# Work moved between places in two engine programs: slot matmuls, index arithmetic and the passage to the expert blocks

## The chip, the cores and the metric

The kernel runs on one core of a Trainium2 chip. The metric is the device time of one execution in microseconds. Five engines run their own instruction queues beside one another: TensorE (PE), VectorE (DVE), ScalarE (ACT), GpSimd (POOL) and SyncE (SP), which here only starts DMAs. They wait for one another by semaphores.

## The reference, cut to what matters

```
x: [32 sequences, 256 tokens, 128]
xn  = layernorm(x)
out = x + attention(xn) + experts(xn)

attention, per sequence (4 heads, keys 32 wide, values 64 wide, chunks of 64):
    q, k, v, g = xn @ Wq, xn @ Wk, xn @ Wv, xn @ Wg
    decay = cumulated log_sigmoid(xn @ Wgk + bgk) / 16
    o  = causal (q k^T * exp(decay differences)) v     # with a state carried on
    on = o * rsqrt(mean(o*o) + eps) * gnorm_w
    attention = (on * g * sigmoid(g)) @ Wo

experts (8), per token, the one with the largest router probability:
    h = gelu(xn @ w1[e] + b1[e]);  y = h @ w2[e] + b2[e]
    experts = probability * y
```

## The kernel before

**Three stages.** The first loads x, transposes it and works out norm statistics, decays and router logits. The second, the attention stage, takes the 32 sequences one by one, two to a turn of a loop. The third takes the tokens, sorted by expert into 71 blocks of 128 rows, eight to a turn.

**A step of the attention stage** (sequence s) on TensorE, in this order: transpose of the keys (L778), query and key projections of s+1 (L757), scores of s (L790), output projection of s-2 (L859), value and gate projections of s+1 (L771, six matmuls of 512 columns), state of s (L814), outputs of s (L825, L839), transpose of the normalized rows of s-1 (L851). ScalarE turns the results into decays (L1148), tanh (L1130), copies (L1139, L1122, L1164) and squares (L1157). Vector, in its own order: gate (L1546), low part of x (L1331), mean square (L1471, L1475), probabilities (L1509), decayed keys (L1515), gated outputs (L1521), scaled queries (L1494), normalized rows (L1529), copy of the state (L1537), residual (L1554). GpSimd takes the inverse root of the mean squares (L561) and masks the decays (L554). Scores of s wait for the gate of s, since they share a PSUM bank, and the value projections of s+1 wait for the first half of the probabilities of s.

**The sort in between.** Beside sequences 2 to 8, small work finds each token's place: TensorE counts tokens and makes their slots (`count_tokens`, `count_totals`, `block_ends`, `slots`, L737 to L742), Vector reads these and works out positions and the expert of each block (`read_ends`, `slots_to_positions`, `past_ends` L1455, `count_past` L1459, `block_experts` L1462). These are hooked into Vector's step at named places: `aside` (ahead of the probabilities), `behind_keys`, `read` (behind the state's copy) and `behind` (at the end). From step 5 to 29 GpSimd also places the rows: each of 64 indirect DMAs (L577) writes 128 rows to sorted memory; `placed_by` sets two or three a step. SP loads the sorted rows (L461) once all placements have landed.

**A block of the last stage**: Vector copies the expert's first-layer weights and biases (`copy_w`, L1669) and normalizes the gathered rows (`norm_rows`, L1676); TensorE transposes them (L956), ScalarE copies the transpose (L1263), TensorE runs the first layer (L965), ScalarE the gelu (L1274), TensorE the second layer (L977), for which it reads the expert's number from memory into a register of its queue (L983); Vector adds the bias and weighs (L1685, L1687), and GpSimd adds the rows to the output with an indirect DMA (`scatter`, L619). The scatters begin only once the attention results of all sequences are stored (SP, L397), because they add to the same rows. `weigh` also copies the row numbers (L1683).

**Orders written out by hand.** There is no planner. Where the attention stage ends and the blocks begin, the code lists each engine's calls by hand: `transpose_on(last, 1)`, `project_out(last, 1)` and `residual(last, 1)` are the last sequence's, `layer1(0, j)`, `layer2(0, j)`, `weigh(0, j)` those of block j.

Of the kernel before, what the change touches and what calls it, by code (L numbers as in the profile page):

```python
# [33 lines left out]
def turn(i, j, d, n):  # L34

    return i + (j + d) // n, (j + d) % n
# [27 lines left out]
def build_layer(nc, x, Wq, Wk, Wv, Wg, Wgk, bgk, Wo, gnorm_w, gate_w, w1, b1, w2, b2, out):  # L64
# [18 lines left out]
    R = 8  # L83
# [21 lines left out]
    with ExitStack() as ctx:  # L105
# [533 lines left out]
        def _(pe):  # L639
# [222 lines left out]

            def step(i, j, extra=None, ahead_of_outputs=None):
                first_keys(i, j)
                proj_qk(*turn(i, j, 1, 2))
                scores(i, j)
                project_out(*turn(i, j, -2, 2))
                if extra:
                    extra()
                proj_vg(*turn(i, j, 1, 2))  # L870
                state(i, j)
                if ahead_of_outputs:
                    ahead_of_outputs()
                outputs(i, j)
                transpose_on(*turn(i, j, -1, 2))
# [63 lines left out]
            step(1, 1, extra=count_totals)  # L939
            step(2, 0, extra=block_ends, ahead_of_outputs=slots)  # L940
            step(2, 1)
# [40 lines left out]
            def expert_of(b):  # L982
                return pe.value_load(be[0:1, bass.ds(b, 1)], min_val=0, max_val=EXP - 1)  # L983

            def block_step(i, j):
                layer1(i, j)
                e = expert_of(i * R + j - 1)
                if not (isinstance(i, int) and i * R + j + 1 >= BLOCKS):
                    transpose_rows(*turn(i, j, 1, R))
                layer2(*turn(i, j, -1, R), e)  # L990

# [16 lines left out]
            transpose_rows(0, 2)  # L1008
            layer1(0, 2)
            transpose_on(last, 1)  # L1010
            transpose_rows(0, 3)
            layer2(0, 1, expert_of(1))
            project_out(last, 1)
            for j in range(3, R):
                block_step(0, j)
            for i in range(1, TURNS - 1):
# [8 lines left out]
        def _(act):  # L1025
# [261 lines left out]
            copy_oT(last, 0)  # L1287
            copy_rows(0, 1)
            copy_rows(0, 2)
            gelu(0, 1)  # L1290
            copy_oT(last, 1)
# [12 lines left out]
        def _(dve):  # L1304
# [251 lines left out]

            def step(i, j, aside=None, behind_keys=None, read=None, behind=None):
                s = i * 2 + j
# [4 lines left out]
                if inside(i, j, -1, SEQS):  # L1563
                    mean_square(*turn(i, j, -1, 2))
                if aside:
                    aside()
                if inside(i, j, 0, SEQS):
                    probs(i, j)
                    decay_k(i, j)
                if behind_keys:  # L1570
                    behind_keys()
                if inside(i, j, -1, SEQS):
# [70 lines left out]
            dve.wait_ge(act_decay, 2 * DECAY_N)  # L1643
            step(2, 0, aside=weights, behind_keys=read_ends, behind=slots_to_positions)
            step(2, 1, aside=past_ends)
            step(3, 0, aside=count_past)
            step(3, 1, aside=block_experts)
            step(4, 0)
            step(4, 1)
# [65 lines left out]
            e = expert_of(0, 3)  # L1715
            mean_square(last, 1)
            gated(last, 1)
            residual(last, 0)
            normed(last, 1)
            norm_rows(0, 3)  # L1720
            copy_w(0, 3, e)
            e = expert_of(0, 4)
            weigh(0, 0)
            e = block_step(0, 1, e)
            residual(last, 1)
            for j in range(2, R):
                e = block_step(0, j, e)
# [17 lines left out]
def placed_by(s):  # L1745

    n = 0
    for k in range(PLACE_FROM, min(s, PLACE_TO) + 1):
        n += 3 if k % 2 == 0 or k in (PLACE_FROM, PLACE_TO) else 2
    return n  # L1750
# [26 lines left out]
```

## Time and profile before

| | us |
|---|---|
| median of 3 runs | 389.69 (388.78 to 390.25) |
| the profiled execution, its own time | 390.25 |
| its span on the core | 388.5 |

| engine | busy us | share of the span |
|---|---|---|
| TensorE | 367.9 | 95% |
| VectorE | 312.5 | 80% |
| ScalarE | 291.5 | 75% |
| GpSimd | 276.0 | 71% |

The shares are means over all stages. In a timeline each row is one instruction or a merged group: its start, how long it took, engine and line, what it writes and reads, and in brackets how long the engine stood idle before it and which instruction ended the wait. The chain of waits starts at the last instruction and follows back, at each step, to what released it; a row of it is a start, a time on the chain, and the instruction.

### The profile page before, as it was taken

Reading aid. Unit: us, or ns where it says so; the run is one execution under the profiler, and the core shown is the slowest. Engines: PE = TensorE matmul, PEld = TensorE weight load, DVE = VectorE, ACT = ScalarE, POOL = GpSimd, SP = SyncE. Lnnn points to the kernel's source line nnn. Section 1 sums busy time; section 2 is a strip of 40 time slices with the busy share of each in tenths; the row PEclk is TensorE's granted clock in tenths of the full one; section 3 lists DMA queues with packets and bytes.
Section 4 is the critical chain, followed back from the end, with each engine's and each line's share of the span. In section 5 each row is a group of like instructions: output and inputs, shape, how many; then the busy total and the mean of one; then the engine's idle time right before and its main releaser. Section 6 shows DMA issues by size and latency. Waiting matters only on the chain.

```text
span 388.5 us, 13868 instructions
## 1 busy us (share of the span) xinstructions
PE 367.9 (95%) x3947; PEld 318.3 (82%) x3947; DVE 312.5 (80%) x859; ACT 291.5 (75%) x889; POOL 276.0 (71%) x245
## 2 busy tenths in 40 slices
PE   6997899999999999999999999999999999999980
PEld 5665677778787888888887877999999999999980
DVE  4898799988889889898889888777768778777750
ACT  3798886879898888989898985676666666666650
POOL 8002453788788888888888873288888888888883
PEclk9998999999999999999999999999999999999995
DMA  8945679556665536665663522255555555555430
GB/s 229 241 157 150 202 228 339 142 175 187 175 205 162 159 127 172 165 196 185 174 187 121 169 57 69 52 71 73 74 66 70 66 70 72 68 72 75 60 32 0
DMA packets 59106, 51.45 MB, mean 132 GB/s; under 512 B 7200, under 2 KB 51392, under 8 KB 59072
## 3 DMA queue, kind: packets, MB, share of 16 engines
q1 hardware_dynamic: 45936, 42.07, 38.6%
q0 software_dynamic: 12272, 8.54, 15.6%
q10 hardware_dynamic: 864, 0.40, 0.4%
q8 instruction: 20, 0.33, 0.3%
q14 instruction: 14, 0.11, 0.1%
HBM read 33.14 MB, written 18.30 MB: 132 GB/s over the span
## 4 chain that ended last, share of the span: by engine, by line
PE 82%; DVE 6%; ACT 4%; issue 3%; POOL 2%; DMA 2%; SPq 0%; DVEq 0%; ACTq 0%; POOLq 0%
PE psVG L965 16%; PE psA L977 16%; PE psVG L771 11%; PE psT L859 8%; PE psO L825 7%; PE psQK L757 5%; PE psT L851 4%; PE psVG L790 4%; PE psO L839 3%; PE psKS L814 3%; ACT E L1148 2%; POOL out_dram L619 2%; DMA x_all<-in_L_attn_x_dram 2%; PE psA L647 1%; DVE stats L1313 1%
## 5 line engine op out<-in xcount | busy, mean ns | idle before, releaser
L619 POOL DMA_INDIRECT out_dram<-yw,sidx x71 | 111.9, 1577 | 28.8 <-DVE yw L1687 10.3
L1148 ACT ACTIVATE E<-gcB,ngc 128x128 f32<-128x128 f32 x256 | 78.3, 394 | 0.0
L577 POOL DMA_INDIRECT sorted_rows<-x_all,pos_i x64 | 63.9, 998 | 13.4 <-issue 9.8
L561 POOL TENSOR_TENSOR rms<-msn,neg_half 128x8 f32<-128x8 f32 x32 | 53.5, 1673 | 24.5 <-DVE msn L1475 20.9
L554 POOL TENSOR_SCALAR_AFFINE_SELECT E<-E 128x1024 f32<-128x1024 f32 x32 | 35.1, 1097 | 37.4 <-ACT E L1148 28.6
L1130 ACT ACTIVATE th<-psVG,x_all 128x256 f32<-128x256 f32 x64 | 26.8, 470 | 21.4 <-PE psVG L771 20.7
L825 PE MATMUL psO<-v_sb,pr 128*64 128x64 f32 x1024 | 36.3, 225 | 2.7 <-DVE pr L1504 2.7
L977 PE MATMUL psA<-xT_all,v_sb 128*128 x288 | 38.1, 275 | 0.4 <-DVE yb L1685 0.4
L965 PE MATMUL psVG<-xgT,gcB 128*128 128x128 f32 x288 | 38.0, 275 | 0.0
L977 PE MATMUL psA<-xT_all,th 128*128 x280 | 37.5, 277 | 0.1
L825 PEld LDWEIGHTS psO<-v_sb,pr 128*64 128x64 f32 x1024 | 34.8, 141 | 3.4 <-issue 3.2
L965 PE MATMUL psVG<-xgT,E 128*128 128x128 f32 x280 | 37.1, 275 | 0.4 <-ACT xgT L1263 0.4
L859 PE MATMUL psT<-wo_sb,oT 128*128 128x128 f32 x256 | 36.9, 287 | 0.3 <-ACT oT L1164 0.3
L977 PEld LDWEIGHTS psA<-xT_all,v_sb 128*128 128x128 f32 x288 | 35.0, 192 | 0.6 <-issue 0.6
L965 PEld LDWEIGHTS psVG<-xgT,gcB 128*128 128x128 f32 x288 | 35.0, 192 | 0.0
L977 PEld LDWEIGHTS psA<-xT_all,th 128*128 128x128 f32 x280 | 34.0, 192 | 0.8 <-issue 0.6
L965 PEld LDWEIGHTS psVG<-xgT,E 128*128 128x128 f32 x280 | 34.1, 192 | 0.6 <-ACT xgT L1263 0.6
L859 PEld LDWEIGHTS psT<-wo_sb,oT 128*128 128x128 f32 x256 | 31.0, 191 | 4.1 <-ACT oT L1164 0.5
L1546 DVE SCALAR_TENSOR_TENSOR gate<-th,psVG 128x512 f32<-128x512 f32 x32 | 22.0, 686 | 9.9 <-ACT v_sb L1139 9.8
L771 PE MATMUL psVG<-w_hi,x_hi 128*128 128x512 f32 x64 | 28.0, 437 | 1.6 <-DVE pr L1509 0.9
L1263 ACT COPY xgT<-psQK 128x128 f32<-128x128 f32 x36 | 9.5, 265 | 24.2 <-PE psQK L956 24.2
L1676 DVE TENSOR_SCALAR xgn<-xg 128x128 f32<-128x128 f32 x71 | 27.1, 381 | 0.0
(209 smaller groups left out, 951.3 us busy)
## 6 DMA issues: line engine op xcount, KB each, us to landing
gcB<-decay_rows SPq DMA_DIRECT2D x32, 512.0 KB, 4.5
sorted_rows<-blank SPq DMA_DIRECT2D x12, 396.0 KB, 5.7
xg<-sorted_rows SPq DMA_DIRECT2D x71, 66.0 KB
x_all<-in_L_attn_x_dram SPq DMA_DIRECT2D x16, 256.0 KB, 5.7
out_dram<-res SPq DMA_DIRECT2D x32, 128.0 KB
eqB<-decay_exp_rows SPq DMA_DIRECT2D x32, 64.0 KB
w1b<-in_L_ffn_w_dram SPq DMA_DIRECT2D x8, 256.0 KB
xT_all<-in_L_ffn_w_dram SPq DMA_DIRECT2D x32, 64.0 KB
```

Of the source, the lines that this page charges most:

```text
L554: nc.gpsimd.affine_select(out=E[j][:], in_=E[j][:], pattern=[[0, 2 * H], [1, P]], compare_op=ALU.is_ge, fill=0.0, base=0, channel_multipli ...
L561: nc.gpsimd.tensor_tensor(rms[:], msn[:], neg_half[:, 0:2 * H], ALU.pow).then_inc(rms_ready, 1)
L577: nc.gpsimd.indirect_dma_start(out=sorted_dram, out_offset=bass.IndirectOffsetOnAxis(ap=pos_i[:, t:t + 1], axis=0), in_=x_all[:, t, :], in ...
L619: nc.gpsimd.indirect_dma_start(out=out_rows, out_offset=bass.IndirectOffsetOnAxis(ap=sidx[j][:], axis=0), in_=yw[j][:], in_offset=None, bo ...
L771: last = nc.tensor.matmul(psVG[:, k, :], xp[:, k * P:(k + 1) * P], wp[:, 2 * P:], start=(n == 0), stop=(n == 2))
L825: nc.tensor.matmul(psO[c * P // 2:(c + 1) * P // 2, k * HV + h * DV:k * HV + (h + 1) * DV], pr[:, h // 2, t:t + P // 2], v_sb[j][:, k, h * ...
L859: last = nc.tensor.matmul(psT[:, k * D:(k + 1) * D], oT[:, 2 * k + a, :], wo_sb[:, a, :], start=(a == 0), stop=(a == 1))
L965: last = nc.tensor.matmul(psVG[:, j % 2, c * P:(c + 1) * P], wbuf[j % 4][:, c * P:(c + 1) * P], xgT[j % 2][:], start=True, stop=True)
L977: last = nc.tensor.matmul(psY[j % 2][:, 0:D], hid[j % 2][:, c, :], w2_sb[:, bass.ds(e, 1), c, :].rearrange("p a d -> p (a d)"), start=(c = ...
L1130: last = nc.scalar.activation(th[:, k, :], psVG[:, k, HV:2 * HV], ACT.Tanh, scale=x_all[:, bass.ds(s * 2 + k, 1), D + 2:D + 3].rearrange(" ...
L1148: last = nc.scalar.activation(E[j][:, k, h * P:(h + 1) * P], gcB[j][:, k * H + h, :], ACT.Exp, bias=ngcf[:, bass.ds((s * 2 + k) * H + h, 1)])
L1676: nc.vector.tensor_scalar(xgn[j % 4][:], xg[j][:, 0:D], xg[j][:, D + 2:D + 3], xg[j][:, D + 3:D + 4], ALU.mult, ALU.add).then_inc(xgn_read ...
```

## The change

Five edits: (1) TensorE's `slots` in step 4 stands ahead of `state` instead of behind it. (2) On Vector the `aside` work stands behind the decayed keys instead of ahead of the probabilities; the place `behind_keys` is gone, and `read_ends` moves behind the state's copy; `past_ends`, `count_past` and `block_experts` move to later places. (3) GpSimd places two groups instead of three in step 5 and three instead of two in step 27. (4) In the passage, TensorE runs the first layer of block 2 and the row transpose of block 3 after `project_out(last, 1)`, not around `transpose_on(last, 1)`; ScalarE runs the gelu of block 1 ahead of the row copy of block 2. (5) There Vector runs the weight copy and row norm of block 3 ahead of the last normalized rows, and `residual(last, 1)` ahead of what belongs to block 1's step.

```diff
@@ TensorE
-            def step(i, j, extra=None, ahead_of_outputs=None):
+            def step(i, j, extra=None, behind_vg=None):
...
                 proj_vg(*turn(i, j, 1, 2))
+                if behind_vg:
+                    behind_vg()
                 state(i, j)
-                if ahead_of_outputs:
-                    ahead_of_outputs()
                 outputs(i, j)
...
-            step(2, 0, extra=block_ends, ahead_of_outputs=slots)
+            step(2, 0, extra=block_ends, behind_vg=slots)
...
-            def block_step(i, j):
+            def block_step(i, j, back=True):
                 layer1(i, j)
-                e = expert_of(i * R + j - 1)
+                if back:
+                    e = expert_of(i * R + j - 1)
                 if not (isinstance(i, int) and i * R + j + 1 >= BLOCKS):
                     transpose_rows(*turn(i, j, 1, R))
-                layer2(*turn(i, j, -1, R), e)
+                if back:
+                    layer2(*turn(i, j, -1, R), e)
...
             layer1(0, 1)
             transpose_rows(0, 2)
-            layer1(0, 2)
             transpose_on(last, 1)
-            transpose_rows(0, 3)
             layer2(0, 1, expert_of(1))
             project_out(last, 1)
-            for j in range(3, R):
-                block_step(0, j)
+            for j in range(2, R):
+                block_step(0, j, back=(j > 2))
@@ ScalarE
             copy_rows(0, 1)
+            gelu(0, 1)
             copy_rows(0, 2)
-            gelu(0, 1)
             copy_oT(last, 1)
@@ Vector
                 if inside(i, j, -1, SEQS):
                     mean_square(*turn(i, j, -1, 2))
-                if aside:
-                    aside()
                 if inside(i, j, 0, SEQS):
                     probs(i, j)
                     decay_k(i, j)
-                if behind_keys:
-                    behind_keys()
+                if aside:
+                    aside()
...
-            step(2, 0, aside=weights, behind_keys=read_ends, behind=slots_to_positions)
-            step(2, 1, aside=past_ends)
-            step(3, 0, aside=count_past)
-            step(3, 1, aside=block_experts)
-            step(4, 0)
+            step(2, 0, aside=weights, read=read_ends, behind=slots_to_positions)
+            step(2, 1)
+            step(3, 0, behind=past_ends)
+            step(3, 1, behind=count_past)
+            step(4, 0, aside=block_experts)
...
             residual(last, 0)
+            copy_w(0, 3, e)
+            norm_rows(0, 3)
             normed(last, 1)
-            norm_rows(0, 3)
-            copy_w(0, 3, e)
             e = expert_of(0, 4)
             weigh(0, 0)
-            e = block_step(0, 1, e)
             residual(last, 1)
-            for j in range(2, R):
+            for j in range(1, R):
                 e = block_step(0, j, e)
@@ GpSimd's placements
-        n += 3 if k % 2 == 0 or k in (PLACE_FROM, PLACE_TO) else 2
+        n += 3 if k % 2 == 0 or k >= PLACE_TO - 2 else 2
```

## Rows read from the trace of the kernel before

**Rows 1.** Chain of waits, 45 to 92 us: start, us on the chain, instruction

```profile
62.58 1.64 PE psVG L771 x6
...
66.00 1.08 PE psO L825 x32
...
70.72 1.65 PE psVG L771 x6
...
77.60 1.66 PE psVG L771 x6
```

**Rows 2.** Chain of waits, 210 to 232 us, a step of the steady loop

```profile
222.85 1.40 PE psVG L771 x6
```

**Rows 3.** Timeline of GpSimd, scatters of blocks 0, 56 and 70 of 71

```profile
249.83 1.79 POOL L619 DMA_INDIRECT out_dram<-yw,sidx  x1 [7.52 <-DVE yw L1687]
...
355.49 1.56 POOL L619 DMA_INDIRECT out_dram<-yw,sidx  x1 [0.30 <-DVE sidx L1683]
...
381.53 1.56 POOL L619 DMA_INDIRECT out_dram<-yw,sidx  x1 [0.30 <-issue]
```

**Rows 4.** Timeline of Vector, weighed rows of block 56

```profile
352.87 0.29 DVE L1687 TENSOR_SCALAR yw<-yb,xg 128x128 f32<-128x128 f32 x1
```

**Rows 5.** Line L619, 248 to 250 us: queue instruction, ns min/median/max, first and last start

```profile
L619 POOLq MOVE  x2: 29/29/29, 249.0 to 249.7; - x2
```

**Rows 6.** Timeline of Vector, 64 to 77 us, steps 4 to 6

```profile
64.74 0.42 DVE L1537 TENSOR_TENSOR S_sb<-psKS,headmask 128x256 f32<-128x256 f32 x1
...
66.03 0.42 DVE L1419 TENSOR_TENSOR slot_f<-psA,onehot 128x256 f32<-128x256 f32 x1 [0.21 <-PE psA L742]
...
67.44 0.69 DVE L1546 SCALAR_TENSOR_TENSOR gate<-th,psVG 128x512 f32<-128x512 f32 x1
...
76.16 0.66 DVE L1459 TENSOR_REDUCE be_f<-isge 128x71 f32<-128x497 f32 x1
```

**Rows 7.** Timeline of TensorE, scores of step 5 and projections in step 6

```profile
68.85 0.38 PE L790 MATMUL psVG<-qk_sb 32*128 32x128 f32 x2
...
77.60 0.50 PE L771 MATMUL psVG<-w_hi,x_hi 128*128 128x512 f32 x1 [0.34 <-DVE pr L1509]
```

**Rows 8.** Timeline of Vector, probabilities in a steady step

```profile
102.15 0.69 DVE L1509 TENSOR_TENSOR pr<-psVG,E 128x512 f32<-128x512 f32 x1 [0.34 <-PE psA L790]
```

**Rows 9.** Timeline of GpSimd, root behind step 27, placement of step 28

```profile
215.32 1.67 POOL L561 TENSOR_TENSOR rms<-msn,neg_half 128x8 f32<-128x8 f32 x1 [0.68 <-DVE msn L1475]
...
218.53 0.96 POOL L577 DMA_INDIRECT sorted_rows<-x_all,pos_i  x1 [0.30 <-DVE on L1529]
```

**Rows 10.** Chain of waits, 240 to 252 us, the passage to the blocks

```profile
242.34 0.12 PE psQK L956
...
242.81 1.16 PE psVG L965 x8
243.97 0.44 PE psT L851 x4
...
244.63 1.16 PE psA L977 x8
...
247.69 0.89 PE psA L977 x8
...
249.58 0.89 PE psA L977 x8
```

**Rows 11.** Timeline of Vector, 232 to 247 us, the passage to the blocks

```profile
232.21 0.92 DVE L1669 COPY gcB<-w1b 128x644 f32 x1
...
242.77 0.69 DVE L1529 TENSOR_TENSOR on<-og,rms 128x512 f32<-128x512 f32 x1 [0.86 <-POOL rms L561]
...
243.63 0.49 DVE L1669 COPY E<-w1b 128x644 f32 x1
...
246.72 0.42 DVE L1554 TENSOR_TENSOR res<-psT,x_all 128x256 f32<-128x256 f32 x1 [0.28 <-PE psT L859]
```

**Rows 12.** Line L983, 243 to 244.6 us: TensorE's queue reads an expert's number

```profile
L983 PEldq TENSOR_LOAD <-be x1: 310/310/310, 243.8 to 243.8; - x1
```

More of the change, by code:

```diff
@@ L1555, in residual, with step @@
                                         ALU.add).then_inc(res_ready, 1)
-            def step(i, j, aside=None, behind_keys=None, read=None, behind=None):
+            def step(i, j, aside=None, read=None, behind=None):
                 s = i * 2 + j
```

## The prediction

> **What bounds the kernel now.** I read the chain of waits in order of time first. From 45 to 230 us it runs almost wholly on TensorE, one sequence after another; a step's six value/gate projections take 1.40 us there when nothing interrupts the engine [rows 2]. In the first steps of that stretch they take 1.64 to 1.66 us: the engine had run dry ahead of them and refills for about 0.25 us, and at 77.60 it had also waited [rows 1]. So a wait of TensorE costs its own length and a quarter of a microsecond.
>
> The second view is GpSimd's timeline. The block stage looks bound by TensorE in the shares, but the 71 scatters stand back to back, with only the 0.30 us between two that every one has: first start 249.83, last 381.53, a mean distance of 131.70 / 70 = 1.881 us [rows 3]. TensorE's own pace is nearly the same: the second layers of two blocks that follow each other start at 247.69 and 249.58, 1.89 apart [rows 10]. Scatter 56 starts at 355.49, and its row was ready at 352.87 + 0.29 = 353.16 [rows 3, 4]: a backlog of 2.33 us. Block 56 is the first of a turn of Vector's loop, where Vector falls back a little; of the stage's 71 blocks it has the least backlog. So the end is set by when the scatters start, and that is by the store of the last attention result: Vector's last residual ends at 246.72 + 0.42 = 247.14, GpSimd's queue gets past its wait at 249.0, the scatter begins at 249.83 [rows 11, 5, 3]. From residual to scatter 2.69 us, of which 0.8 lies behind the wait. That 0.8 us is also the least backlog that a scatter can have without GpSimd standing still.
>
> **Part 1, slots ahead of state (step 4).** No matmul is added or removed. Between the projections' end, 62.58 + 1.64 = 64.22, and the outputs at 66.00 lie the four state and twelve slot matmuls, 1.78 us in either order [rows 1]. What moves is Vector. Its copy of the state stood at 64.74, under the slot matmuls; now the state comes out at about 66.00, so the copy starts at 66.05. Behind it wait the read of the block ends, a residual and the slot reads, for which I take the distances between starts in the same view, 0.34, 0.19 and 0.33. First slot read 66.05 + 0.34 + 0.19 + 0.33 = 66.91, second 67.25 (before: 66.03). From second read to the next gate it was 67.44 - 66.03 = 1.41 [rows 6], so the gate of step 5 starts at 68.66 instead of 67.44 and ends at 69.35. TensorE's scores of step 5 wait for it; they stood at 68.85 [rows 7]. Loss: 69.40 - 68.85, **0.55 us**.
>
> **Part 2, the index work of Vector moved.** The comparison, count and cast leave the place ahead of the probabilities. In step 5 this pays back at once: the probabilities come 0.7 us sooner after the gate, TensorE's projections no longer wait and don't refill. They start at 70.66 + 0.55 = 71.21 and take 1.40, end 72.61, against 70.72 + 1.65 = 72.37 [rows 1, 2]: 0.24 late. In step 6 the count (0.66 at 76.16, 0.7 with the wait for its result) is gone from in front of the probabilities [rows 6]. TensorE had idled 0.34 [rows 7] and refilled to 77.60 + 1.66 = 79.26. Now: without wait 77.60 - 0.34 = 77.26, plus 0.24, plus 1.40 = 78.90. So from here on the kernel is **0.36 us ahead**. The comparison and the count, 0.7 us each, now stand ahead of the gates of steps 7 and 8, where Vector idles 0.3 for the value copy and again 0.34 ahead of the probabilities [rows 8], and TensorE needs these another 0.3 later: just covered. If not, 0.1 plus a refill of 0.25, once or twice. Sum early: -0.36, bounds -0.6 and +0.55 (nothing recovered).
>
> **Part 3, a placement from step 5 to step 27.** It costs 0.96 + 0.30 [rows 9]. In step 5 GpSimd has room. In step 27 it idles 0.68 ahead of the root [rows 9]; steps 26 to 29 now hold three each, so GpSimd is up to 0.5 late there and the last placement 0.35 late. The first gathered rows are needed only after Vector's weight copy of 232.21, which no load feeds [rows 11], and SP's loads of these rows, which wait for the last placement, come 0.35 late at most. I take 0, bounds 0 and +0.4.
>
> **Part 4, the passage to the blocks.** The last normalized rows are ready at 242.77 + 0.69 = 243.46 either way, since Vector waited 0.86 for GpSimd's root; the weight copy (0.49) and row norm (0.34) now lie inside that wait [rows 11]. Before, TensorE filled the time with the first layer of block 2 (242.81, 1.16) and transposed at 243.97. Now it has nothing between the row transpose at 242.34 and 243.52: an idle 1.1 us [rows 10]. Then four transposes (0.6), the second layer of block 1, the output projection. The second layer needs an expert number read into a register on TensorE's own queue. That read stood at 243.8 and took 0.31 [rows 12], and the matmuls began at 244.63 [rows 10], 0.83 after it. The transposes are queued at once when the rows are ready, so the read now starts at about 243.6 and the second layer at 244.43: only 0.2 earlier, though the transposes end at 244.1. Everything behind keeps its distance: residual 246.52, first scatter 249.63, **-0.20 us**. Bounds: -0.57 (read hidden), +0.15 (below).
>
> The rows transpose of block 3 now stands directly in front of its first layer, with nothing in between: transpose, copy by ScalarE, restart, as at 242.34 to 242.81, 0.47, and 0.27 of refill (1.16 against 0.89) [rows 10]. TensorE: second layer 244.43 + 1.16 = 245.59, projection to 246.48, first layer of block 2 to 247.37, transpose 0.11, layer 3 from 247.95 to 249.11, transpose 0.11, second layer of block 2 at about 249.25, against 247.69 [rows 10]: **1.56 us later**. This is the price of what was brought forward, and the backlog pays it: at block 56 it was 2.33, becomes 2.33 - 1.56 - 0.20 = 0.57, and the least is 0.8. So GpSimd stands still about **0.25 us** there. The earlier turns begin with a larger backlog, so I take nothing there.
>
> **Sum.** -0.36 - 0.20 + 0.25 = -0.3 us. The profiled execution took 390.25 (span 388.5 and 1.75 around it), the highest of the three; it would take 389.95. Against the median of 389.69 that is **389.4 us**.
>
> Vector's weight copy of the same form took 0.92 at 232.21, beside GpSimd's mask, and 0.49 at 243.63, beside no GpSimd work [rows 11]. It now stands beside the last root: if held to its end, the rows come 0.15 late. The Trainium skill says so too (GPSIMD Engine Reference, Key points): the two engines share their SBUF interfaces, and Vector's two-port modes contend. By that rule the sum would be -0.15; if the root leaves the port free, -0.3.
>
> Of the register read the Trainium skill gives a floor of some 600 ns (DMA: Bandwidth & Descriptors, Latency and other measured facts). The trace has 0.83 to the matmul, so the measurement decides; by the page's figure alone the first scatter would be 0.2 earlier still. Both agree that such a read is not free, and it speaks against this order.
>
> **Rivals.**
> 1. *The register read is hidden.* For: in steady blocks nothing is lost at it. Against: here the queue stands before it until 243.46. Then scatters start 0.57 earlier, TensorE is only 1.2 late, and block 56 again limits: -0.8 in all, 388.9.
> 2. *The stall in step 5 stays* (slower). For: the gate of step 5 is 1.2 us late, and the root and the mask follow from it, GpSimd's work too. Against: the removed count is longer than what is left. It decides if the probabilities of step 6 miss 77.1. Then +0.55 stays: +0.55 - 0.20 + 0.25, with 390.2 as a time.
> 3. *The blocks' compute becomes the bound.* For: only 0.57 of backlog left at block 56. If the restart costs 0.5 more than I worked out, or Vector falls back further at boundaries, GpSimd waits 0.5 to 1 at each such place: +0.8, 390.5.
> 4. *The scatters' own pace shifts.* The last one took 1.56, with the 0.30 ahead of it 1.86, the first 1.79 [rows 3]: it depends on how they fall against Vector's work, and with a backlog changed by 1.8 they fall elsewhere. As far above the mean of 1.881 as 1.86 lies below it is 1.90. 70 distances at 1.86 are 130.2, at 1.90 133.0, against 131.7: -1.5 to +1.3 on the forecast, 387.9 to 390.7.
>
> **Chances.** Forecast 0.43, rival 1 0.15, rival 2 0.14, rival 3 0.12, rival 4 0.16. The range goes from rival 4's low end to its high end with a little for the median's own scatter (388.78 to 390.25 before): 387.7 to 391.0. About 0.5%, 1.9 us, is what a measurement of this kernel tells from no change. Below 387.7 I put 0.10 (rival 4's low end, with 1), above 391.6 0.05, the rest 0.85.
>
> **What would show it.** Right: TensorE waits some 0.5 us ahead of the scores of step 5 and not ahead of the projections of step 6; in the passage it idles over 1 us ahead of the last transposes and again ahead of block 3's first layer; the last residual 0.2 earlier relative to the rows of 243.46; a smaller backlog of scatters, nearly none at block 56. Wrong: a residual over 0.5 earlier (rival 1), a later projection in step 6 (2), scatters that wait for Vector in many blocks (3), or a mean distance far from 1.88 (4).

## The result and the profile after

| | before | after |
|---|---|---|
| median of 7 runs | 389.47 us (388.56 to 391.76) | 392.53 us (392.00 to 393.25) |
| profiled execution, its own time / span | 390.25 / 388.5 | 391.56 / 389.8 |

The ratio is 1.0074, with an interval of 1.0048 to 1.0099: the change makes the kernel slower by 0.74%. The forecast of 389.4 and its range up to 391.0 were wrong, in size and in sign.

The shares tell nothing of it. From the page of after, busy us, share of the span and count of each engine:

```profile
PE 368.7 (95%) x3947; PEld 319.1 (82%) x3947; DVE 312.4 (80%) x859; ACT 292.0 (75%) x889; POOL 277.2 (71%) x245
```

So the two traces are cut at events that both have. The profiled pair differs by 1.31 us; what comes before step 3, which the change doesn't touch, was 1.14 us shorter in after's execution (the projections in step 2 stand at 47.82 against 48.96; this part varies from run to run). From there on after is 2.45 us longer. The projections for sequence s+1 run in step s, so those for sequences 4 and 9 run in steps 3 and 8:

| stretch | before | after | difference | predicted |
|---|---|---|---|---|
| projections for sequence 4 to those for sequence 9 | 34.43 | 35.29 | +0.86 | -0.36 |
| to those for sequence 26 | 107.11 | 107.15 | +0.04 | 0 |
| to those for sequence 31 | 31.58 | 32.23 | +0.65 | 0 |
| to the end of the last normalized rows | 13.20 | 13.23 | +0.03 | 0 |
| to the end of the last residual | 3.68 | 3.44 | -0.24 | -0.20 |
| to the first scatter | 2.68 | 2.69 | +0.01 | 0 |
| first to last scatter | 131.70 | 132.82 | +1.12 | +0.25 |

**The early stretch.** Vector after, steps 4 to 7 (answers to [rows 6]), and first the comparison in before:

```profile
69.18 0.67 DVE L1455 TENSOR_TENSOR isge<-iota_f,ends 128x497 f32<-128x497 f32 x1
```

```profile
64.87 0.42 DVE L1537 TENSOR_TENSOR S_sb<-psKS,headmask 128x256 f32<-128x256 f32 x1 [0.87 <-PE psKS L814]
...
67.47 0.69 DVE L1546 SCALAR_TENSOR_TENSOR gate<-th,psVG 128x512 f32<-128x512 f32 x1
...
79.15 1.94 DVE L1455 TENSOR_TENSOR isge<-iota_f,ends 128x497 f32<-128x497 f32 x1
81.13 0.69 DVE L1546 SCALAR_TENSOR_TENSOR gate<-th,psVG 128x512 f32<-128x512 f32 x1
...
86.39 0.66 DVE L1459 TENSOR_REDUCE be_f<-isge 128x71 f32<-128x497 f32 x1
```

GpSimd beside it:

```profile
79.45 1.10 POOL L554 TENSOR_SCALAR_AFFINE_SELECT E<-E 128x1024 f32<-128x1024 f32 x1
80.73 1.21 POOL L577 DMA_INDIRECT sorted_rows<-x_all,pos_i  x1 [0.18 <-issue]
...
86.03 1.10 POOL L554 TENSOR_SCALAR_AFFINE_SELECT E<-E 128x1024 f32<-128x1024 f32 x1
```

And the chain of waits of the same stretch (answers to [rows 1]):

```profile
67.59 0.67 issue
68.26 0.38 PE psVG L790 x2
...
70.08 1.64 PE psVG L771 x6
...
76.61 1.47 PE psVG L771 x6
...
79.58 1.52 DVE isge L1455
81.13 0.70 DVE gate L1546
```

The state copy idled 0.87 us, and the scores of step 5 waited 0.67 for the gate: part 1 as forecast. Two steps later stands what was not: the comparison, 0.67 us long in before, took 1.94, from 79.15 to 81.09. GpSimd's mask ran from 79.45 to 80.55 over it. The gate behind it starts at 81.13 and the chain leaves TensorE for it. The count at 86.39 lay beside a mask too (86.03 to 87.13) and took its 0.66: it reads one array where the comparison reads two.

**The last steps.** Vector's low part of x in steps 28 and 29, in before and in after, and GpSimd's mask in each step of after:

```profile
213.77 0.42 DVE L1331 TENSOR_TENSOR x_lo<-xT_all,x_hi 128x256 fp32r<-128x256 f32 x1
...
220.07 0.82 DVE L1331 TENSOR_TENSOR x_lo<-xT_all,x_hi 128x256 fp32r<-128x256 f32 x1
```

```profile
213.53 1.14 DVE L1331 TENSOR_TENSOR x_lo<-xT_all,x_hi 128x256 fp32r<-128x256 f32 x1
220.14 1.16 DVE L1331 TENSOR_TENSOR x_lo<-xT_all,x_hi 128x256 fp32r<-128x256 f32 x1
```

```profile
213.28 1.10 POOL L554 TENSOR_SCALAR_AFFINE_SELECT E<-E 128x1024 f32<-128x1024 f32 x1
...
219.90 1.11 POOL L554 TENSOR_SCALAR_AFFINE_SELECT E<-E 128x1024 f32<-128x1024 f32 x1
```

With three placements in each of steps 26 to 29 GpSimd is late, and its mask slides over this operation, which also reads two arrays. The mean squares and the probabilities stand behind it in Vector's order, and TensorE's projections wait for the probabilities; so the chain of waits leaves TensorE in step 28 and in step 29 (answers to [rows 2], where a group that hadn't run dry took 1.40):

```profile
213.53 0.47 DVE x_lo L1331
...
215.61 0.70 DVE pr L1509
...
216.36 1.68 PE psVG L771 x6
...
222.97 1.67 PE psVG L771 x6
```

**The passage.** TensorE after, 243 to 250 us (answers to [rows 10]):

```profile
243.95 0.65 PE L851 MATMUL psT<-ident,on 128*128 128x128 f32 x4 [1.10 <-DVE on L1529]
244.82 1.15 PE L977 MATMUL psA<-xT_all,th 128*128 x8 [0.22 <-issue]
...
248.22 1.16 PE L965 MATMUL psVG<-xgT,E 128*128 128x128 f32 x8 [0.36 <-ACT xgT L1263]
...
249.35 1.15 PE L977 MATMUL psA<-xT_all,v_sb 128*128 x8
```

The idle time of 1.1, the 0.2 us behind the transposes for the register read, the second idle time ahead of block 3: all as written. In this execution everything here stands 0.43 us later than in before (the rows are ready at 243.89 instead of 243.46), so block 2 is compared from the rows: its weighed rows come 7.29 us behind them instead of 5.77, 1.52 later.

**The scatters.** GpSimd after, first scatter, blocks 23 to 26, and the last (answers to [rows 3]); then Vector's weight copies beside them:

```profile
250.02 1.65 POOL L619 DMA_INDIRECT out_dram<-yw,sidx  x1 [7.27 <-DVE sidx L1681]
...
293.70 1.55 POOL L619 DMA_INDIRECT out_dram<-yw,sidx  x1 [0.30 <-issue]
295.55 1.81 POOL L619 DMA_INDIRECT out_dram<-yw,sidx  x1 [0.30 <-DVE yw L1685]
297.67 1.59 POOL L619 DMA_INDIRECT out_dram<-yw,sidx  x1 [0.30 <-issue]
...
382.84 1.55 POOL L619 DMA_INDIRECT out_dram<-yw,sidx  x1 [0.30 <-issue]
```

```profile
293.70 0.53 DVE L1667 COPY gcB<-w1b 128x644 f32 x1
295.12 0.49 DVE L1667 COPY gcB<-w1b 128x644 f32 x1
296.79 0.49 DVE L1667 COPY E<-w1b 128x644 f32 x1
298.69 0.49 DVE L1667 COPY E<-w1b 128x644 f32 x1
```

The idle times between the 71 scatters sum to 21.3 us in before and after alike, 0.30 each: GpSimd waited for no block. What grew is the scatters, and only some of them: it hangs on where a weight copy starts against the scatter. At 295.55 one starts 1.24 us behind the scatter's start (296.79), and the scatter takes 1.81; at 297.67 one starts 1.02 behind (298.69), and it takes 1.59; at 293.70 one starts with it and one 1.42 behind, and it takes 1.55. In the profiles of all the kernels here together 101 scatters took over 1.65 us, and beside every one of them a copy starts either 0.03 to 0.13 us ahead of the scatter or 1.05 to 1.24 us behind its start; of the scatters with such a copy only two took less, 1.62 and 1.55. The page's group of these scatters, in before and in after:

```profile
L619 POOL DMA_INDIRECT out_dram<-yw,sidx x71 | 111.9, 1577 | 28.8 <-DVE yw L1687 10.3
```

```profile
L619 POOL DMA_INDIRECT out_dram<-yw,sidx x71 | 113.0, 1592 | 28.6 <-DVE sidx L1681 10.3
```

Over 1.65 us were 5 scatters before and 8 after, from 1.57 to 1.65 they were 15 and 26. The backlog at block 56 was 1.27 us instead of 2.33 (forecast 0.57). Copies come every 1.91 us and undisturbed scatters every 1.86, so a copy drifts by about 0.05 us a block against the scatters and passes through the two costly positions more or less often. The backlog sets where this drift starts. That last step is worked out from these rows, and no run tests it by itself.

### The profile page after: what moved, and what is told of

Its sections match the earlier page's. It is cut to its first block, busy times and chain, and to the rows that moved or that the text cites. A ratio compares the mean times of both kernels' runs of the same rounds, so it can differ in the third digit from the quotient of the medians.

```text
span 389.8 us, 13865 instructions
## 1 busy us (share of the span) xinstructions
PE 368.7 (95%) x3947; PEld 319.1 (82%) x3947; DVE 312.4 (80%) x859; ACT 292.0 (75%) x889; POOL 277.2 (71%) x245
## 4 chain that ended last, share of the span: by engine, by line
PE 79%; DVE 7%; ACT 4%; issue 3%; SPq 3%; POOL 1%; DMA 1%; DVEq 0%; ACTq 0%; POOLq 0%
PE psA L977 16%; PE psVG L965 16%; PE psVG L771 11%; PE psT L859 7%; PE psO L825 7%; PE psQK L757 4%; PE psT L851 4%; PE psVG L790 4%; PE psO L839 3%; SPq L355 2%; PE psKS L814 2%; ACT E L1148 2%; DVE stats L1313 1%; PE psKS L956 1%; PE psQK L956 1%
## 5 line engine op out<-in xcount | busy, mean ns | idle before, releaser
L619 POOL DMA_INDIRECT out_dram<-yw,sidx x71 | 113.0, 1592 | 28.6 <-DVE sidx L1681 10.3
L825 PEld LDWEIGHTS psO<-v_sb,pr 128*64 128x64 f32 x1024 | 34.9, 141 | 3.3 <-issue 3.2
L1674 DVE TENSOR_SCALAR xgn<-xg 128x128 f32<-128x128 f32 x71 | 26.2, 369 | 0.0
L1263 ACT COPY xgT<-psKS 128x128 f32<-128x128 f32 x35 | 9.3, 266 | 21.7 <-PE psKS L956 21.7
```

The costliest lines, as they stand in the source:

```text
L619: nc.gpsimd.indirect_dma_start(out=out_rows, out_offset=bass.IndirectOffsetOnAxis(ap=sidx[j][:], axis=0), in_=yw[j][:], in_offset=None, bo ...
L825: nc.tensor.matmul(psO[c * P // 2:(c + 1) * P // 2, k * HV + h * DV:k * HV + (h + 1) * DV], pr[:, h // 2, t:t + P // 2], v_sb[j][:, k, h * ...
L1674: nc.vector.tensor_scalar(xgn[j % 4][:], xg[j][:, 0:D], xg[j][:, D + 2:D + 3], xg[j][:, D + 3:D + 4], ALU.mult, ALU.add).then_inc(xgn_read ...
```

## The experiments

Each ratio is to the kernel before, run in turn with it on the same chip. Chips differ: x10 to x12 ran where before took 389.7 us, as in the result, the others on chips where it took 394.7 to 396.1. On the slower chips a steady step of the attention stage takes 6.50 us instead of 6.30, and the last five steps 32.77 with the old placements instead of 31.58; so times are compared within a group only, and the slower group has no trace of before itself: x4, x5 and x7 stand for it where their edits don't reach. The stretches, in us from one profiled execution each:

| | ratio (interval) | sequences 4 to 9 | sequences 26 to 31 | rows to residual | scatters |
|---|---|---|---|---|---|
| *before* | | 34.43 | 31.58 | 3.68 | 131.70 |
| *after* | 1.0074 (1.0048 to 1.0099) | 35.29 | 32.23 | 3.44 | 132.82 |
| x10 | 1.0013 (0.9992 to 1.0034) | 34.42 | 31.59 | 3.30 | 131.72 |
| x11 | 0.9997 (0.9973 to 1.0021) | 34.15 | 31.59 | 3.69 | 131.70 |
| x12 | 0.9975 (0.9953 to 0.9997) | 33.70 | 31.58 | 3.69 | 131.71 |
| *slower chips* | | | | | |
| x1 | 1.0043 (1.0013 to 1.0073) | 35.06 | 33.42 | 3.43 | 133.33 |
| x2 | 1.0078 (1.0051 to 1.0106) | 36.25 | 32.75 | 3.44 | 133.43 |
| x3 | 1.0023 (0.9997 to 1.0048) | 35.27 | 33.45 | 3.68 | 131.74 |
| x4 | 1.0034 (1.0009 to 1.0059) | 34.62 | 32.77 | 3.44 | 133.40 |
| x5 | 1.0025 (1.0000 to 1.0051) | 34.61 | 32.77 | 3.69 | 133.59 |
| x6 | 1.0061 (1.0033 to 1.0088) | 35.26 | 33.40 | 3.01 | 133.33 |
| x7 | 0.9959 (0.9932 to 0.9986) | 34.66 | 32.79 | 3.68 | 130.52 |
| x9 | 1.0026 (1.0000 to 1.0053) | 35.53 | 32.76 | 3.68 | 131.91 |
| x13 | 0.9975 (0.9947 to 1.0003) | 35.01 | 32.84 | 3.66 | 133.41 |
| x14 | 1.0007 (0.9983 to 1.0031) | 35.59 | 32.90 | 3.68 | 131.52 |

Inside the first of these stretches, the start of the last projection matmul of steps 5, 6, 7 and 8, in us from that of step 3 (its projections begin at 54.7 in after and 55.9 in before):

| | to 5 | to 6 | to 7 | to 8 |
|---|---|---|---|---|
| *before* | 14.82 | 21.72 | 28.06 | 34.43 |
| *after* | 15.32 | 21.67 | 28.91 | 35.29 |
| x12 | 14.65 | 20.98 | 27.32 | 33.70 |
| x11 | 14.71 | 21.47 | 27.81 | 34.15 |
| *slower chips:* x4, in this stretch the kernel before | 14.81 | 21.73 | 28.26 | 34.62 |
| x1 | 15.32 | 22.08 | 28.72 | 35.06 |
| x2 | 15.31 | 22.08 | 29.92 | 36.25 |
| x3, x6 | 15.31 | 21.66 | 28.91 | 35.27 |
| x9 | 15.33 | 22.60 | 29.20 | 35.53 |
| x13 | 14.66 | 21.46 | 28.63 | 35.01 |
| x14 | 15.73 | 22.66 | 29.22 | 35.59 |

**x1: after, the comparison back in step 5.**

```diff
-            step(2, 1)
-            step(3, 0, behind=past_ends)
+            step(2, 1, aside=past_ends)
+            step(3, 0)
```

> The changed kernel with one thing undone in part: Vector's comparison (L1455) runs in step 5, behind the decayed keys, instead of at the end of step 6. Theory: in the changed kernel it took 1.94 us instead of 0.67 because it stood beside GpSimd's mask and a placement, and TensorE's scores of step 7 waited for the gate behind it. Here it takes under 0.8, TensorE does not wait at those scores, and from the projections of step 4 to those of step 8 the time falls from 22.2 us to 21.3; the whole is 0.9 us faster than the changed kernel, about 391.6. Rival: the stretch is slow because of the slots ahead of the state; then the comparison may be short, but the stretch stays at 22 us or more and the whole at 392.4.

The comparison took 0.67 again, and from step 6 to 7 the projections were 6.64 apart instead of the 7.25 of x3 and x6. But step 6 came 0.42 later, since the comparison is in front of the probabilities again. What is left is 0.2, not the 0.9 of the theory: moving it back mends the long comparison and gives up what its move had gained.

**x2: after, with the placements of before.**

```diff
-        n += 3 if k % 2 == 0 or k >= PLACE_TO - 2 else 2
+        n += 3 if k % 2 == 0 or k in (PLACE_FROM, PLACE_TO) else 2
```

> The changed kernel with the placements as before (three in step 5, two in step 27). Theory: with three placements in each of steps 26 to 29 GpSimd's mask slides onto Vector's low part of x, which took 1.14 and 1.16 us at 213.5 and 220.1 instead of 0.42 and 0.82, so the probabilities came late and TensorE waited and refilled ahead of two groups of projections. Here these low parts take 0.42 and 0.82 again, and TensorE does not wait; 0.6 us faster than the changed kernel, about 391.9. Rival: GpSimd has room for them and the two waits come from elsewhere; then they stay and the time stays at 392.5.

The last five steps took 32.75 instead of the 33.40 to 33.45 of x1, x3 and x6, and this operation of steps 28 and 29 fell back from 0.95 to 1.01 in x1 and x3 to these:

```profile
218.96 0.42 DVE L1331 TENSOR_TENSOR x_lo<-xT_all,x_hi 128x256 fp32r<-128x256 f32 x1
225.40 0.68 DVE L1331 TENSOR_TENSOR x_lo<-xT_all,x_hi 128x256 fp32r<-128x256 f32 x1
```

The placements' 0.65 us is shown. The whole wasn't faster for it: the third placement, back in step 5, makes GpSimd later there (its mask beside the comparison starts 1.0 us later against step 3 than in x3), step 6 comes 0.42 later than in x3, the comparison took 2.06, and the stretch from sequence 4 to 9 took 36.25, 1.0 more than in x3. So edit 3 had a gain in step 5 too, which I had priced at nothing, once the slots' order has made that step late.

**x3: after, the passage of before (edits 4 and 5 undone). x4: before, with edits 4 and 5 alone.**

> The changed kernel with the passage to the blocks (TensorE, ScalarE and Vector) as before the change. Theory: the passage brings the first scatter 0.2 to 0.3 us forward and puts the blocks' compute 1.6 us back; the backlog of scatters is smaller by both, and with a small backlog GpSimd's scatters fall on Vector's copies and are stretched: the 70 distances summed to 132.8 instead of 131.7 us. Here the sum is about 131.7 and the whole 0.9 us faster than the changed kernel, about 391.6. Rival: the sum varies from run to run, whatever the backlog; then undoing the passage only loses its 0.2 us: 392.7, with a sum near 132.8 or anywhere from 131.5 to 133.

> The kernel before with the passage alone changed (edits 4 and 5). Theory of the backlog: TensorE idles 1.1 us ahead of the last transposes, the residual comes 0.2 to 0.3 us sooner, the backlog of scatters at block 56 falls from 2.3 to about 1.3 (the whole stage keeps one), the 70 distances sum to 132.8 and the time is 0.9 us over before, about 390.4. Rival (the pace is by chance): only the 0.2 of the earlier first scatter is seen, 389.3.

In these two, rows to residual and scatters go with the passage: 3.68 and 131.74 with the old one, 3.44 and 133.40 with the new. x4 alone is slower than before by 0.34%, though its first scatter comes 0.2 us earlier.

**x5: before, the first layer of block 3 computed three times.** It delays TensorE's blocks by 1.8 us, about as the new passage does, and changes nothing else.

```diff
-                for c in range(FC):
+                for c in list(range(FC)) * (3 if isinstance(i, int) and b == 3 else 1):
```

> The kernel before, with the first layer of block 3 computed three times over (the same matmuls into the same place), so that the compute of all blocks from there on comes 1.8 us later, and nothing else changes: the last residual and the first scatter stay where they are. Backlog theory: the smaller backlog alone stretches the scatters; their 70 distances sum to 132.8 to 133.4 us instead of 131.7, the backlog at block 56 falls to 1.8 or less, and the kernel is 1.1 to 1.7 us slower than before, although GpSimd never waits for a block. Rival (the stretch comes with the changed order of Vector or ScalarE in the passage, or by chance): the sum stays at 131.7 and the time at that of before.

The scatters took 133.59 us in the profiled execution, with nine over 1.65 us, and in the page:

```profile
L619 POOL DMA_INDIRECT out_dram<-yw,sidx x71 | 113.8, 1603 | 28.9 <-issue 14.6
```

Idle times again 0.30 each. So later blocks are enough for the longer scatters; Vector's order in the passage isn't needed for them. The theory's backlog was missed at block 56, 2.29 us instead of 1.8 or less: it was 1.73 at block 16 (before 3.59), and the longer scatters built it up again.

**x6: after, the expert number of block 1 read ahead of the transposes.**

```diff
-            transpose_on(last, 1)
-            layer2(0, 1, expert_of(1))
+            e = expert_of(1)
+            transpose_on(last, 1)
+            layer2(0, 1, e)
```

> The changed kernel, but TensorE's queue reads the expert number of block 1 ahead of the last transposes instead of behind them. Theory of the read (0.83 us from its start to the matmul): TensorE, which idles there anyway, has the number when the rows come; the second layer of block 1 starts 0.60 to 0.65 us after the last normalized rows instead of 0.93, and the last residual ends 3.1 us after them instead of 3.44. Rival (the second layer waits for the gelu or for the transposes, not for the register): 0.93 and 3.44 stay. The scatters stay stretched, sum 133, so the whole is at most 0.3 us faster than the changed kernel.

TensorE behind the last rows:

```profile
250.46 0.66 PE L851 MATMUL psT<-ident,on 128*128 128x128 f32 x4 [1.11 <-DVE on L1530]
```

From the rows to the second layer it was 0.55 instead of 0.93, and the residual came 0.43 sooner (3.01). The read, in the queue behind the wait, is what cost it.

**x7: before, the weight copy cut from 644 to 8 columns from block 8 on.** It leaves out the blocks' own weights there.

> The kernel before, with Vector's weight copy in the block stage cut from 644 columns to 8 from block 8 on: it leaves the right expert's weights out, all else runs. Theory: scatters are stretched by what Vector does through both SBUF inputs or in its fast copy beside them, the 0.48 us copy most of all. Without it the distances come to 1.86 each, a sum of 130.2 to 130.6 instead of 131.7, and at most three scatters take over 1.65 us: 1.1 to 1.5 us faster than before. Rival (the stretch has its cause in GpSimd or the DMA queue): the sum stays within 0.3 of 131.7.

```profile
L619 POOL DMA_INDIRECT out_dram<-yw,sidx x71 | 110.7, 1560 | 28.9 <-issue 11.0
```

One scatter over 1.65 us, the first, which stands before the cut copies; the sum fell to 130.52, which is 70 distances of 1.865. The kernel was 0.41% faster. Taking the copy away takes the stretching away: this shows the cause of the long scatters.

**x9: after, with x1's and x2's edits and the old passage. x11: x9, with the slots behind the state again.**

> The changed kernel with the comparison in step 5, the placements as before and the passage as before: what is left is the slots ahead of the state and the index work behind the keys. If three terms explain the slowdown (comparison 0.9, placements 0.6, scatters 1.1 to 1.7), it is within 0.5 us of before: scatters sum to 131.7, the last five steps to 32.75, and the stretch from the projections of step 4 to those of step 9 is 34.4 to 34.9. Rival (the slots order costs the 0.55 us of the gate and is not paid back): that stretch is 35.0 to 35.2 and the kernel 0.5 us slower than before.

> As the repaired kernel with the old passage, but TensorE's slots stand behind the state again; what is left of the change is the index work behind the decayed keys. Theory of the gate: the slots ahead of the state held Vector's copy of the state for 0.88 us and made the scores of step 5 wait 0.67 us; here the copy does not wait, the gate of step 5 starts a microsecond sooner against the projections, and the stretch from the projections of step 4 to those of step 9 falls from 35.53 to 34.6 us or less. Rival (the index work behind the keys costs it, by the weights and the comparison ahead of the normalized rows): the stretch stays above 35.2.

x9 took 35.53 from sequence 4 to 9, above the 34.4 to 34.9 of its theory and the 35.0 to 35.2 of its rival, where the order of before takes 34.6 on such a chip, with the state copy again behind an idle time of 0.88 and the comparison at 0.67. x11 took 34.15, 0.3 less than before on its chip; its time is that of before. The slots' order is the only edit between the two, and up to step 5 it is 15.33 against 14.71, 0.62 us. By step 6 it is 1.13 (22.60 against 21.47), where the order of before takes the same on both kinds of chip (21.72 and 21.73).

**x10: before, with x6's early read.**

> The kernel before, but TensorE's queue reads the expert number of block 1 ahead of the last transposes. Theory: the second layer of block 1 follows the row transpose without a gap, 0.12 us of wait and 0.27 of refill go, so the last residual ends 3.3 us after the last normalized rows instead of 3.68; residual and compute come forward by the same 0.39 us, so the backlog of scatters and their sum (131.7) stay, and the kernel is 0.4 us faster than before. Rival (an earlier residual always eats backlog and is given back): the sum rises above 132.5 and the time is that of before or slower.

Rows to residual fell from 3.68 to 3.30. A tenth of a per cent can't be seen in the time, and wasn't (1.0013, with 1 inside the interval): inconclusive there.

**x12: before, the index work of Vector alone in its late places.**

```diff
-            step(2, 1, aside=past_ends)
-            step(3, 0, aside=count_past)
-            step(3, 1, aside=block_experts)
-            step(4, 0)
+            step(2, 1)
+            step(3, 0, behind=past_ends)
+            step(3, 1, behind=count_past)
+            step(4, 0, aside=block_experts)
```

> The kernel before with one edit: comparison, count and cast at the end of steps 6 and 7 and ahead of the probabilities of step 8 instead of steps 5 to 7. Theory: the comparison reads two operands from SBUF and stands beside GpSimd's mask and placement at the end of step 6, so it takes 1.9 us instead of 0.67 and the gate behind it holds up TensorE's scores; the stretch from the projections of step 4 to those of step 9 grows from 34.62 by 0.3 to 0.9 us (0.9 for the held scores, less what the earlier places had cost). The count, which reads one operand, takes 0.66 beside a mask. Rival (the comparison was long only because the slots had shifted GpSimd's work): it takes 0.67 to 0.8 and the stretch is 34.4 or less.

Vector, then GpSimd:

```profile
77.26 0.67 DVE L1455 TENSOR_TENSOR isge<-iota_f,ends 128x497 f32<-128x497 f32 x1
```

```profile
77.93 1.10 POOL L554 TENSOR_SCALAR_AFFINE_SELECT E<-E 128x1024 f32<-128x1024 f32 x1
```

The comparison ended as the mask began: the theory missed and its rival held. The stretch took 33.70, 0.73 less than before, and the kernel was faster, 0.9975. Against x12, on a chip of the same pace, after is 0.67 later at step 5, 0.69 at step 6 and 1.59 at step 7. From step 3 on its comparison starts 0.68 later than in x12 and its mask only 0.31 later, so the two overlap, and that costs the last 0.90. The 0.69 isn't the slots' order alone: after also has the block ends and the weights in other places and a placement less in step 5.

**x13: x12 with the early read. x14: before, with slots ahead of the state alone.**

> The kernel before with two edits that each were run alone: the comparison, count and cast at the end of steps 6 and 7 and behind the decayed keys of step 8 (their places in the changed kernel), and expert_of(1) read ahead of the transposes of the last normalized rows. Theory (the two gains stand in different stretches and add): the projections of step 4 to those of step 9 take 33.7 us (before 34.4), from the last normalized rows to the last residual 3.3 us (before 3.68), first to last scatter 131.7 us as before; the whole 1.1 us less than before, ratio 0.997. Rival (what the scatters take hangs on how they fall against Vector's copies, so an earlier start shifts it): 33.7 and 3.3 as above, but the scatters' 70 distances take over 132.3 us, and the ratio is 0.999 or above.

> The kernel before with one edit: slots ahead of state in step 4; all of Vector's index work where it was. Theory (the slots' place by itself costs TensorE a wait that isn't given back): Vector idles some 0.9 us ahead of the state copy of step 4, the gate and the scores of step 5 come 0.6 to 0.7 us late, and with the comparison still in front of the probabilities the projections of step 5 start late by as much; the projections of step 4 to those of step 9 take 35.0 to 35.2 us instead of 34.4, ratio 1.0015 to 1.002. Rival (TensorE already ran dry in steps 5 and 6, so the wait is covered by the stalls that are there): 34.4 to 34.6 us and ratio 1.000; then the changed kernel's loss of 0.8 us there comes from the order of Vector's work and not from the slots.

x14: slots alone took 35.59 against 34.6, 1.0 us, more than expected, 0.92 of it by step 5. Vector, then TensorE:

```profile
65.09 0.42 DVE L1537 TENSOR_TENSOR S_sb<-psKS,headmask 128x256 f32<-128x256 f32 x1 [1.13 <-PE psKS L814]
```

```profile
68.28 0.38 PE L790 MATMUL psVG<-qk_sb 32*128 32x128 f32 x2 [0.46 <-issue]
...
70.78 0.47 PE L771 MATMUL psVG<-w_hi,x_hi 128*128 128x512 f32 x1 [0.68 <-DVE pr L1509]
```

The wait for the gate, and another for the probabilities, which follow the comparison there. Its time, 1.0007, has both theories' values in its interval; the stretch decides, not the time.

x13 missed both of its stretches. Vector's comparison, and GpSimd's mask:

```profile
78.33 1.87 DVE L1456 TENSOR_TENSOR isge<-iota_f,ends 128x497 f32<-128x497 f32 x1
```

```profile
78.56 1.10 POOL L554 TENSOR_SCALAR_AFFINE_SELECT E<-E 128x1024 f32<-128x1024 f32 x1
```

On this chip the comparison starts 0.47 us later from step 3 on than in x12 and the mask at the same place, 0.2 us into the comparison, without the slots' edit: 35.01 instead of the 33.70 of x12. x12's gain hangs on how the engines fall against one another there, and doesn't carry from chip to chip in the profile. The two gains don't add either: from the last projections to the last residual it is 16.88 in before, 16.49 in x10, 16.52 in x12 and 16.54 in x13; x12's rows come 0.36 earlier (as they do in x3, x9, x11 and x13; why, stays open), so that its transposes and its read pass straight behind the first layer of block 2. And with the old passage the scatters took 133.41. The ratio of 0.9975 is the same as x12's, with 1 just inside the interval, but no gain of x13 is shown. The last projection matmul of step 3, up to which the edits of x12 to x14 change nothing, starts between 54.74 and 57.92 us in the profiles. From there to the end of its time x12 took 332.0 us against 333.1 in before, which agrees with its ratio; x13 took 340.0 against the 338.9 of x14 on the same chip, which itself is slowed by the slots. x12 is the best version found. (Its expectation puts x13's cast behind the decayed keys of step 8; the edit leaves it ahead of the probabilities, as in x12.)

## Why the prediction was wrong

**Part 1 was right** by the mechanism written: TensorE waited 0.67 us ahead of the scores, which came 0.55 late as forecast (68.26 with the 1.14 of the shorter start is 69.40). The prediction counts twelve slot matmuls where the code has ten; its 1.78 us is read from the rows and doesn't hang on that.

**Part 2 failed at "just covered".** It had after 0.24 late at step 5 and 0.36 ahead at step 6; it was 0.50 late (the refill of 70.08, 1.64, stayed) and 0.05 ahead. That is a miss of 0.3. The large one is in step 7: the comparison, entered at 0.67 us from a row that had no mask beside it, took 1.94, its gate came late, and after fell 0.85 behind. The alternative that I gave, "0.1 plus a refill", had the place right and the size wrong: it let the comparison be late but not long. By the runs on chips of one pace the +0.86 is made of -0.73 for the late index work (x12), +0.69 up to step 6 for the slots and what else differs there, and +0.90 for the long comparison. What the slots' order costs hangs on what stands around it: alone it was 1.0 (x14), and 1.13 by step 6 between x11 and x9.

**Part 3 failed at the 0.** I priced the moved placement by GpSimd's own idle time and asked who waits for GpSimd; nobody does for long. But the mask slid over an operation of Vector's which became 0.3 to 0.7 us longer, in two steps: +0.65, above the bound of +0.4; x2 shows it. The trace of before had the sign of it: the same low part took 0.97 at 74.47, with the mask over it from 74.05 to 75.15, and 0.82 in a steady step with three placements. The same edit's gain in step 5 (x2 against x3: 0.4 at step 6) was missed too.

The Trainium skill has the rule (GPSIMD Engine Reference, Key points): the engine contends with Vector instructions in a two-port mode *or with two SBUF inputs*. I used its first half, for a copy. Beside the mask the trace agrees (0.91 at 232.61 in after); beside the root, where I used it, it was not borne out, since the copy took 0.48 at 242.22 while the root ran to 242.74. The second half is what the rows of this case show: the comparison 0.67 to 1.94, the low part of x 0.42 to 1.16, while the reduce with one input kept 0.66.

**Part 4 was right in the passage** (-0.24 for -0.20, block 2 later by 1.52 for 1.56) **and wrong at the end**. I took what a smaller backlog costs as a wait at block 56 and entered 0.25; GpSimd never waited. The term is the scatters' own time, +1.12. It also kept the backlog up, 1.27 at block 56 where 0.57 stood. Rival 4 named this, and gave up to +1.3 on the forecast; I gave it 0.16. Alone it ends at 390.7, so it doesn't reach the 392.5 either: parts 2 and 3 had to miss too. The rows that I had for it were there: a first scatter of 1.79 between others of 1.56 [rows 3].

The size of this term stays loose. The sum was 130.5 without the copy, 131.5 to 131.9 in seven of the eight other profiles with the old passage and blocks on time (before, x3, x9 to x12, x14), 133.41 in the eighth (x13), and 132.8 to 133.6 in all six with later blocks (after, x1, x2, x4, x5, x6). In x13 the scatters ran as in before until block 14 and then took another course, with a larger backlog than before (3.54 at block 56), so a small backlog isn't a condition. Which scatters are long is told by the positions of the copies; what sends a whole run through more of them isn't settled, only that all six profiles with later blocks went that way.

Sum of the differences: 2.45 us in the pair of traces from step 2 on, against 3.06 between the medians, 2.9 by the ratio, with its interval of 1.9 to 3.9.

## What to carry to other kernels

Where work is moved on Vector or on GpSimd, write down for each Vector operation with two SBUF inputs, and each wide copy, what GpSimd does in that very time, before and after the move: an operation that was priced with no mask beside it can be three times as long with one (0.67 to 2.06 here). A queue of transfers that never waits can still get slower, so ask of a smaller backlog not only whether it reaches zero but which engine's work the transfers now lie against: a tenth of a microsecond decides here between 1.55 and 1.85. And a reorder that fills one wait (the slots under the projections) should be followed to the next reader of what it delays, here Vector's copy of the state, with everything queued behind it.

## What the runs showed of the hardware

- GpSimd's mask (1.10 us) keeps its length; beside it Vector's comparison of two SBUF arrays (128x497) goes from 0.67 to between 1.87 and 2.06 (after, x2, x3, x6, x13), and a subtraction of 128x256 (the low part of x) from 0.42 to 1.16. In before, x1, x9, x11, x12 and x14 the comparison had no mask over it and took 0.67.
- A placement's DMA issue that follows such a mask took 1.21 us instead of 0.97 where the comparison ran over its first 0.36 us too (80.73 in after).
- A scatter takes 1.55 us on GpSimd undisturbed, 1.78 to 2.00 where a 128x644 copy of Vector's starts 0.03 to 0.13 us ahead of it, and from 1.57 rising to 1.81 where one starts 1.0 to 1.24 us behind its start. Elsewhere a copy costs it at most 0.07 us.
- TensorE's read of an expert number costs 0.38 to 0.43 us when it stands behind a wait (x6, x10), and nothing that can be seen when it is queued ahead of it.
- Chips differ by more than this change: before took 389.5 to 396.1 us, most of it in the attention stage (6.30 and 6.50 us a step).
